# First attention of a four-part network: the four value passes of a head group stand in pairs, in two slots instead of four

## Chip, cores and metric

One NeuronCore of a Trainium2 chip runs the whole kernel in one launch. The metric is device time in microseconds (us); the median of the runs shown counts. Engines are called PE (TensorE, matrix products and transposes), DVE (VectorE), ACT (ScalarE), POOL (GpSimd) and SP (SyncE, which here issues DMAs). They run side by side, each through its own list of instructions in order, and wait for each other by semaphores.

## What is computed

The network has two blocks, each an attention and a feed-forward part, with a residual sum and a normalisation after each part. The change lies in the first attention alone: causal softmax attention over 4 batch entries, 512 positions, width 256, 16 heads of width 16, with rotary angles on the first four columns of each head.

```python
# x: (4, 512, 256)
qkv = x @ w_qkv + b_qkv                       # 16 heads of q, k, v, 16 wide each
q, k = rotate(q), rotate(k)                   # first 4 columns of each head
scores = where(causal, q @ k.T, -inf)
probs = softmax(scores)
attn = probs @ v                              # the value passes of this case
x = layernorm(x + attn @ w_out + b_out)
# then: the wave feed-forward part, a linear attention, six feed-forward blocks
```

## The kernel before

**Tiling.** A batch entry's 512 positions are four tiles of 128 (`RT` = 4). The heads are taken two at a time, in 8 pairs (`PAIRS`), and two pairs make a group of four heads (`GROUPS` = 4 of them). For each of the four entries, `entry(i, when)` of each engine walks through 8 pairs `p` with 4 slots `r` each, 32 slots in all; below (p,r) is a slot. `when` is "first" for entry 0, "loop" for entries 1 and 2, "last" for entry 3.

**One slot on PE.** `entry` (L954 on) issues, in this order: `score_pass(i, p, r)` (L835), two products, one for each head of the pair, over keys of tile `J_ORDER[r]`, so 512, 128, 384 and 256 columns in slots 0 to 3; `max_pass` (L824), the same two heads of the pair two further on, 128, 256, 384 and 512 columns, of which DVE takes row maxima; at most one `value_pass` (L848); in slot 1 `max_rows` (L858), a transpose of the negated maxima; then `use_work`, whatever the table `WORK_AT` has for the slot: transposes of q and k stacks (`stack`, L878), of the input (`x_T`), of the attention's output (`att_T`) or the normalised rows (`next_T`, all L943), a projection to q, k, v (`project`, L871) or the output projection (`out`, L887); and in slot 3 of even pairs `transpose_outputs` (L864). In some slots `keep_busy` (L952) adds products whose result nobody reads. In the last entry products that prepare the next part (L923, L929) take the place of some of the work.

**Value passes.** `value_pass(i, q, r)` multiplies the probabilities of key tile `J_ORDER[r]` by the values, for the four heads of group q, each head in its own 32 columns of the array: pass 0 has 512 columns, pass 1 128, pass 2 384, pass 3 256. They are called v0, v1, v2, v3 here. A pass is 8 matmuls in the trace (two rounds of four heads). All four add into one bank, `outputs`. v0 waits until ACT has copied the group before; each pass waits for `g_sel`, POOL's causal mask (`select`, L579) of slot r of the odd pair of its group. Group q is pairs 2q and 2q+1; its v0 and v1 stand in slots 2 and 3 of the odd pair, v2 and v3 in slots 0 and 1 of the even pair behind it (for the last group of an entry that is pair 0 of the next entry, and for the last group of all the end of the loop, where v2 and v3 stand together already).

**What orders the work around it.**
- Scores: ACT takes exponentials (L695) of each slot's two score products into `probs`; POOL masks them. A score pass waits until all but the last exponential of the slot before are done (in slot 0: all of them), since three banks are shared.
- Maxima: each head of the pair has one bank. The max pass of a slot waits, head by head, until DVE has taken the maximum (L1104) of the slot before. The maximum pass of slot (p,1) is followed on DVE by `take_rows` (L1118), whose rows SP sends by DMA to `heads_T`; `score_pass` of the next pair's slot 0 waits for that.
- `use_work` has one bank, `work`, and `max_rows`, `stack` and `transpose_outputs` share another, `exchange`. A use waits until its reader is done with the use before. The readers: ACT copies the stacks out (`copy_k` L682, `copy_q` L688) and takes the high part of transposes (`high`, L663 to L667); DVE takes the low part (`low`, L1141) and adds biases of projections (L1153). ACT also builds the next stack's high part (`stack_high`, L674 and L676), POOL its low part (`stack_low`, L585 and L587), and POOL rotates (L564 to L568).
- In slot 0 of even pairs the work is: pair 0 `stack`, pair 2 `att_T`, pair 4 `stack`, pair 6 `project`; in slot 3 of odd pairs: pair 1 `stack`, pair 3 `out`, pair 5 `stack`, pair 7 `project` (entry 0 has no `att_T` and no `out`).

Of the kernel before, what the change touches and what calls it, by code (L numbers as in the profile page):

```python
# [304 lines left out]
def work_table(when):  # L305

    table = {}
    for p, r, kind, arg in WORK_AT:
        if kind in PREVIOUS:
            used = when != "first"  # L310
        else:
            used = when != "last" if kind == "x_T" else of_entry(when, arg[0])
        if used:
            table[p, r] = (kind, arg)
    for p, r, kind, arg in {"first": FIRST_AT, "loop": (), "last": LAST_AT}[when]:
        table[p, r] = (kind, arg)
    return dict(sorted(table.items()))


def group_at(p, r, when):  # L320
    return r == RT - 1 and p % 2 == 0 and (p > 0 or when != "first")
# [39 lines left out]
def attention0(nc, A, g, top):  # L361
# [15 lines left out]
    GROUPS = H // 4  # L377
# [83 lines left out]
    def wait(eng, sem, count):  # L461

        if not isinstance(count, int) or count > 0:
            eng.wait_ge(sem, count)
# [341 lines left out]
    def _(pe):  # L806
        pe.wait_ge(s["ident_in"], 16)

        def max_pass(i, p, t, unit_at):

            if p % UP == 0:

                if unit_at[1] == "before":
                    pe.wait_ge(s["first_copied"], 2 * (t + 1))
                else:
                    key = ("stack", (1 if p else 2, t))
                    pe.wait_ge(s["work_read"], WORK.number(*unit_at, key) + 1)
                    pe.wait_ge(s["ex_read"], EXCHANGE.number(*unit_at, key) + 1)
            for o in range(2):
                n = (i * PAIRS + p) * 2 * RT + 2 * t + o  # L820
                rows = slice(o * SLOT, (o + 1) * SLOT)

                pe.wait_ge(s["v_max"], n + 1)
                pe.matmul(ps[:, o, 0:(t + 1) * P], heads_T[rows, p // UP, 0, p % UP, t * P:(t + 1) * P],  # L824
                          heads_T[rows, p // UP, 1, p % UP, 0:(t + 1) * P], start=True, stop=True).then_inc(s["p_max"], 1)

        def score_pass(i, p, r):
            j = J_ORDER[r]
            if r == 0:
                pe.wait_ge(s[f"m_row{p % 2}"], 32 * (i * (PAIRS // 2) + p // 2 + 1))  # L830

            wait(pe, s["a_exp"], ((i * PAIRS + p) * RT + r) * 2 - (0 if r == 0 else 1))
            for o in range(2):
                rows = slice(o * SLOT, (o + 1) * SLOT)
                pe.matmul(ps[:, score_bank(r, o), 0:COLS[j]], heads_T[rows, p // UP, 1, p % UP, j * P:(j + 1) * P],  # L835
                          heads_T[rows, p // UP, 0, p % UP, j * P:S], start=True, stop=True).then_inc(s["p_score"], 1)

        def value_pass(i, q, r):

            j = J_ORDER[r]  # L840
            if r == 0:
                pe.wait_ge(s["a_out"], i * GROUPS + q + 1)
                if q % 2 == 0:
                    pe.wait_ge(s["g_val"], 2 * RT * i + (q // 2 + 1) * RT)
            pe.wait_ge(s["g_sel"], (i * PAIRS + 2 * q + 1) * RT + r + 1)
            for h in range(4):
                rows = 2 * DH * h
                mm = pe.matmul(outputs[rows:rows + 2 * DH, j * P:S], val[:, j, 4 * q + h, :],  # L848
                               probs[:, h // 2, h % 2, OFF[j]:OFF[j] + COLS[j]],
                               start=(r == 0), stop=(r == RT - 1))  # L850
            if r == RT - 1:
                mm.then_inc(s["p_out"], 1)

        def max_rows(i, when, p, pair):

            pe.wait_ge(s["v_neg"], pair + 3)
            pe.wait_ge(s["ex_read"], EXCHANGE.number(i, when, ("neg", p)))
            pe.transpose(exchange[:, 0:P].bitcast(F32R), neg_max[:, :], ident_r[:, :]).then_inc(s["p_ex"], 1)  # L858

        def transpose_outputs(i, when, q):  # L860
            pe.wait_ge(s["a_out"], i * GROUPS + q + 2)
            pe.wait_ge(s["ex_read"], EXCHANGE.number(i, when, ("group", q if when != "after" else -1)))
            for t in range(RT):
                mm = pe.transpose(exchange[:, t * P:(t + 1) * P], out_T[:, t * P:(t + 1) * P], ident[:, :])  # L864
            mm.then_inc(s["p_ex"], 1)
# [84 lines left out]
        def keep_busy(bank, count):  # L950
            for _ in range(count):
                pe.matmul(bank, wout_h[:, 0, 0:P], wout_h[:, :, :].rearrange("p c d -> p (c d)"), start=True, stop=True)  # L952

        def entry(i, when):  # L954
            table = work_table(when)
            for p in range(PAIRS):
                for r in range(RT):
                    if (i, p, r) != (0, 0, 0):
                        score_pass(i, p, r)
                    if p + 2 < PAIRS:  # L960
                        max_pass(i, p + 2, r, (i, when))
                    elif when != "last":
                        max_pass(i + 1, p + 2 - PAIRS, r, (i, when))

                    if p % 2 and r >= 2:
                        value_pass(i, p // 2, r - 2)
                    elif p % 2 == 0 and r < 2 and p:
                        value_pass(i, p // 2 - 1, r + 2)
                    elif p == 0 and r < 2 and when != "first":
                        value_pass(i - 1, GROUPS - 1, r + 2)  # L970
                    row_next = r == 1 and (p < PAIRS - 1 or when != "last")

                    if row_next and p != 1:
                        max_rows(i, when, p + 1, i * PAIRS + p + 1)
                    if (p, r) in table:
                        use_work(i, when, *table[p, r])
                    if row_next and p == 1:
                        max_rows(i, when, p + 1, i * PAIRS + p + 1)
                    if group_at(p, r, when):
                        transpose_outputs(i, when, p // 2 - 1)  # L980
                    if (p, r) in KEEP_AT[when]:
                        count, use = KEEP_AT[when][p, r]
                        wait(pe, s["work_read"], WORK.number(i, when, use))
                        keep_busy(work, count)
# [47 lines left out]
        pe.wait_ge(s["g_ones"], 1)  # L1032
        pe.wait_ge(s["g_wout"], 1)
        entries(pe, entry)
        for r in range(2, RT):
            value_pass(B - 1, GROUPS - 1, r)
# [1616 lines left out]
```

## Time and profile before

| | us |
|---|---|
| median of 3 runs | 1064.11 (1063.26 to 1064.51) |
| the profiled execution's own time | 1064.57 |
| its span in the trace | 1062.8 |
| first attention's loops, from pair 0 of entry 0 to the last value pass | about 32 to 303 |
| PE busy over the span | 1001.7 (94%) |
| DVE, ACT, POOL busy | 748.1 (70%), 611.1 (57%), 373.8 (35%) |

Between span and time lie 1.8 us that the trace does not cover. PE's busy time counts a matmul from its dispatch to its modelled end, so that matmuls overlap in it and short waits hide in it; the distance from the start of one pass to the start of the next is the better measure of what a pass takes, and it is used below. A bracket at a row's end names the idle time of the engine ahead of it and what ended it.

### The profile page before, as it was taken

To read this page: it belongs to the slowest core of one execution; us is meant where nothing else is said; L and a number is where in the kernel's file an instruction comes from. 1 tells how busy PE (TensorE), PEld (TensorE's weight loads), DVE (VectorE), ACT (ScalarE), POOL (GpSimd) and SP (SyncE) were. 2 spreads that over 40 slices of the span, in tenths; PEclk is the share of its full clock that TensorE was granted. 3 is DMA by queue.
4 is the path that set the end of the run, shared out by engine and by line. 5 is a ranking of instruction groups with operands and counts; after the bars stand their busy time and mean duration, and the time that the engine had idled before them with its cause. 6 is when DMAs were issued, how large, how long until landed. Compare 5 with 4: busy or idle time off the path is not lost.

```text
span 1062.8 us, 18308 instructions
## 1 busy us (share of the span) xinstructions
PE 1001.7 (94%) x6627; PEld 836.2 (79%) x6627; DVE 748.1 (70%) x2042; ACT 611.1 (57%) x1177; POOL 373.8 (35%) x725
## 2 busy tenths in 40 slices
PE   6999999999998898889999999999999999999995
PEld 5555655556667897778989999998999999899995
DVE  5666787777639678967567767667776766677646
ACT  5566667564368576555556665456666545666640
POOL 4454474551221573553622233222223322222600
PEclk9899999999999999999999999999999999999998
DMA  7000010022110010022101011010101101010101
GB/s 247 22 2 21 4 41 1 22 67 74 60 45 4 1 34 9 1 100 80 60 1 41 3 38 41 1 41 1 40 2 40 40 2 40 1 41 1 52 29 40
DMA packets 29234, 36.91 MB, mean 35 GB/s; under 512 B 1780, under 2 KB 26584, under 8 KB 29144
## 3 DMA queue, kind: packets, MB, share of 16 engines
q1 hardware_dynamic: 24872, 31.28, 9.1%
q10 hardware_dynamic: 4272, 4.46, 1.4%
q8 instruction: 53, 0.87, 0.3%
q14 instruction: 37, 0.30, 0.1%
HBM read 31.40 MB, written 4.20 MB: 33 GB/s over the span
## 4 chain that ended last, share of the span: by engine, by line
PE 54%; DVE 5%; ACT 1%; POOL 1%; issue 1%; DMA 1%; SPq 0%; DVEq 0%; POOLq 0%; ACTq 0%
PE ps L1894 25%; PE ps L1877 24%; PE ps L1849 2%; PE ps L1767 1%; PE ps L1818 1%; DVE ln_stats L86 1%; DMA mlp_b<-L_ffn_LN_B 1%; DVE ln_stats L2256 0%; ACT xn L2016 0%; ACT x_b L2037 0%; DVE att L2339 0%; PE ps L1809 0%; DVE xT_l L2298 0%; PE ps L1720 0%; DVE ln_mv L91 0%
## 5 line engine op out<-in xcount | busy, mean ns | idle before, releaser
L2115 ACT ACTIVATE G<-ps,bias_col 128x512 f32<-128x512 f32 x192 | 135.5, 706 | 186.3 <-PE ps L1877 176.8
L1894 PE MATMUL ps<-w_h,G_h 128*128 128x256 f32 x736 | 208.2, 283 | 0.0
L1894 PE MATMUL ps<-w_h,G_l 128*128 128x256 f32 x736 | 207.9, 282 | 0.0
L1894 PE MATMUL ps<-w_l,G_h 128*128 128x256 f32 x736 | 207.8, 282 | 0.0
L2387 DVE TENSOR_TENSOR G_l<-G,G_h 128x512 fp32r<-128x512 f32 x192 | 155.2, 815 | 59.9 <-ACT G_h L2116 59.9
L1696 POOL TENSOR_TENSOR x_a<-xn,mlp_g 128x1024 f32<-128x1024 f32 x20 | 67.6, 3379 | 344.8 <-DVE xn L2417 344.8
L695 ACT ACTIVATE probs<-ps 128x512 f32<-128x512 f32 (+3 forms) x256 | 98.3, 441 | 98.2 <-PE ps L835 97.4
L1877 PE MATMUL ps<-xT_h,w_h 128*128 128x512 f32 x384 | 152.0, 396 | 1.1 <-issue 1.1
L1877 PE MATMUL ps<-xT_h,w_l 128*128 128x512 f32 x384 | 150.6, 392 | 0.0
L1877 PE MATMUL ps<-xT_l,w_h 128*128 128x512 f32 x384 | 150.4, 392 | 0.0
L1104 DVE CUSTOM_DVE_ANT_0 ps<-ps,q_mask 128x128 f32<-128x128 f32 (+3 forms) x256 | 120.7, 512 | 30.6 <-PE ps L824 30.1
L1894 PEld LDWEIGHTS ps<-w_h,G_h 128*128 128x128 f32 x736 | 139.9, 190 | 0.7
L1894 PEld LDWEIGHTS ps<-w_h,G_l 128*128 128x128 f32 x736 | 140.3, 191 | 0.0
L1894 PEld LDWEIGHTS ps<-w_l,G_h 128*128 128x128 f32 x736 | 139.5, 190 | 0.8
L2116 ACT ACTIVATE G_h<-ps,bias_col 128x512 fp32r<-128x512 f32 x192 | 135.0, 703 | 0.0
L2401 DVE TENSOR_TENSOR rsum<-ps,x_a 128x1024 f32<-128x1024 f32 x23 | 28.2, 1225 | 105.4 <-PE ps L1894 105.4
L579 POOL TENSOR_SCALAR_AFFINE_SELECT probs<-probs 128x256 f32<-128x256 f32 x128 | 53.1, 416 | 99.1 <-ACT probs L695 98.4
L1877 PEld LDWEIGHTS ps<-xT_h,w_h 128*128 128x128 f32 x384 | 72.1, 188 | 16.2 <-issue 1.5
L1877 PEld LDWEIGHTS ps<-xT_h,w_l 128*128 128x128 f32 x384 | 72.1, 188 | 15.7
L1877 PEld LDWEIGHTS ps<-xT_l,w_h 128*128 128x128 f32 x384 | 72.2, 188 | 14.9
L2381 DVE TENSOR_TENSOR xT_l<-hs,xT_h 128x512 fp32r<-128x512 f32 x40 | 77.1, 1954 | 2.3 <-ACT xT_h L2101 1.1
L824 PE MATMUL ps<-heads_T 64*128 64x128 f32 (+3 forms) x256 | 56.6, 353 | 5.9 <-DVE top_score L1104 5.7
(303 smaller groups left out, 2120.7 us busy)
## 6 DMA issues: line engine op xcount, KB each, us to landing
w_raw<-L_ffn_W_T SPq DMA_DIRECT2D x12, 1024.0 KB, 5.5
hs<-L_attn_hidden_states SPq DMA_DIRECT2D x8, 512.0 KB, 4.0
x_kept<-hs SPq DMA_DIRECT2D x4, 512.0 KB, 3.9
w_raw<-x_kept SPq DMA_DIRECT2D x2, 1024.0 KB, 5.4
out<-xn SPq DMA_DIRECT2D x3, 512.0 KB, 2.9
w_raw<-L_ffn_ent_w_T SPq DMA_DIRECT2D x1, 1024.0 KB, 9.9
w_raw<-L_ffn_ent_pw SPq DMA_DIRECT2D x1, 1024.0 KB, 12.3
heads_T<-neg_rows SPq DMA_DIRECT2D x64, 2.0 KB
```

The source lines that it names most:

```text
L579: pool.affine_select(diagonal, diagonal, [[0, 2], [1, P]], ALU.is_ge, 0.0, base=0, channel_multiplier=-1).then_inc(s["g_sel"], 1)
L695: act.activation(probs[:, p % 2, o, OFF[j]:OFF[j] + COLS[j]], ps[:, score_bank(r, o), 0:COLS[j]], ACT.Exp).then_inc(s["a_exp"], 1)
L824: pe.matmul(ps[:, o, 0:(t + 1) * P], heads_T[rows, p // UP, 0, p % UP, t * P:(t + 1) * P], heads_T[rows, p // UP, 1, p % UP, 0:(t + 1) * P ...
L1104: v.tensor_tensor_reduce(ps[:, o, 0:(t + 1) * P], ps[:, o, 0:(t + 1) * P], q_mask[:, S - (t + 1) * P:S], 1.0, MASKED, ALU.add, ALU.max, to ...
L1696: pool.tensor_tensor(g.x_a[:, rows, :], xn[:, b % 2, :, :], bcast(g.mlp_g[:, i, :], 1, [P, RT, D]), ALU.mult).then_inc(feed["g_mul"], 1)
L1877: mm = pe.matmul(ps[:, hidden_bank(i, n), :], w[:, c, f * P:(f + 1) * P], x[:, b, c, :], start=(k == 0), stop=(k == 5))
L1894: mm = pe.matmul(ps[:, 4 + t // 2, (t % 2) * D:(t % 2 + 1) * D], x[b % 2][f][:, t * P:(t + 1) * P], w2_chunk(w, f), start=(k == 0), stop=( ...
L2115: act.activation(G32[n % 4], bank, ACT.Gelu, bias=bias)
L2116: act.activation(G_h[b % 2][f], bank, ACT.Gelu, bias=bias).then_inc(feed["a_g"], 1)
L2381: v.tensor_tensor(g.xT_l[:, b, c, :], src, g.xT_h[:, b, c, :].bitcast(F32), ALU.subtract).then_inc(feed["v_T"], 1)
L2387: v.tensor_tensor(G_l[b % 2][f], G32[n % 4], G_h[b % 2][f].bitcast(F32), ALU.subtract).then_inc(feed["v_gl"], 1)
L2401: v.tensor_tensor(g.rsum[:, :, :], ps[:, 4:6, :].rearrange("p a (b c) -> p (a b) c", c=D), g.x_a[:, b * RT:(b + 1) * RT, :], ALU.add).then ...
```

## The change

The call sites of `value_pass` in PE's `entry` move. v1 goes from slot 3 of the odd pair to slot 2, right behind v0; v3 goes from slot 1 of the even pair to slot 0, right behind v2. The passes themselves, their waits, all other engines' programs and the passes at the end of the loop stay as they are.

```diff
-                    if p % 2 and r >= 2:
-                        value_pass(i, p // 2, r - 2)
-                    elif p % 2 == 0 and r < 2 and p:
-                        value_pass(i, p // 2 - 1, r + 2)
-                    elif p == 0 and r < 2 and when != "first":
-                        value_pass(i - 1, GROUPS - 1, r + 2)
+                    if p % 2 and r == 2:
+                        value_pass(i, p // 2, 0)
+                        value_pass(i, p // 2, 1)
+                    elif p % 2 == 0 and r == 0 and p:
+                        value_pass(i, p // 2 - 1, 2)
+                        value_pass(i, p // 2 - 1, 3)
+                    elif p == 0 and r == 0 and when != "first":
+                        value_pass(i - 1, GROUPS - 1, 2)
+                        value_pass(i - 1, GROUPS - 1, 3)
```

## Rows read from the trace of the kernel before

**Rows 1.** Busy time by stretch, entry 1: us; busy by engine; granted clock; DMA, GB/s.

```profile
95.50:158.30 62.80, 59.00 (x443) 36.84 (x441) 49.81 (x189) 41.56 (x106) 34.91 (x96) 1.00 0.06 18
```

**Rows 2.** Waits of PE, 46 to 303.4 us: total us, times, longest.

```profile
PE ps L824 <- DVE top_score L1104: 4.5, 9, 0.9
PE ps L835 <- ACT probs L695: 2.8, 6, 0.7
```

**Rows 3.** Timeline, entry 1, (1,2) to (2,1): start, us, engine, line, operation, tiles, [idle].

```profile
106.91 1.07 PE L848 MATMUL ps<-probs,val 128*32 128x512 f32 x8
...
107.93 0.38 PE L835 MATMUL ps<-heads_T 64*128 64x256 f32 x2
...
108.16 0.54 PE L824 MATMUL ps<-heads_T 64*128 64x512 f32 x2
...
108.63 0.43 PE L848 MATMUL ps<-probs,val 128*32 128x128 f32 x8
108.98 0.54 PE L878 MATMUL ps<-ident_r,k_stack 128*128 128x128 f32 x4
...
109.87 0.14 DVE L1104 DVE_READ_ACCUMULATOR2_ANT top_score<- 128x1 f32 x1
109.87 0.49 PE L835 MATMUL ps<-heads_T 64*128 64x512 f32 x2
...
110.21 0.22 PE L824 MATMUL ps<-heads_T 64*128 64x128 f32 x2
110.35 0.85 PE L848 MATMUL ps<-probs,val 128*32 128x384 f32 x8
...
111.14 0.66 PE L943 MATMUL ps<-ident,att 128*128 128x128 f32 x4
...
112.15 0.64 PE L848 MATMUL ps<-probs,val 128*32 128x256 f32 x8
...
112.46 0.69 DVE L1141 TENSOR_TENSOR att_l<-ps,att_h 128x512 fp32r<-128x512 f32 x1 [1.27 <-ACT att_h L665]
112.72 0.28 PE L858 MATMUL ps<-ident_r,neg_max 128*128 128x128 f32 x1
...
113.20 0.44 PE L871 MATMUL ps<-wqkv_h,x_h 128*128 128x384 f32 x1 [0.21 <-DVE att_l L1141]
```

**Rows 4.** Timeline of PE, the end of entry 3: v1 and v2 without work between.

```profile
301.49 1.07 PE L848 MATMUL ps<-probs,val 128*32 128x128 f32 x16
...
301.73 0.51 PE L848 MATMUL ps<-probs,val 128*32 128x384 f32 x4
```

**Rows 5.** Timeline, entry 1, (4,0) and (4,1): ACT's copy and the next row transpose.

```profile
128.70 0.59 ACT L688 ACTIVATE heads_T<-ps 128x512 fp32r<-128x512 f32 x1
...
129.44 0.28 PE L858 MATMUL ps<-ident_r,neg_max 128*128 128x128 f32 x1
```

**Rows 6.** Timeline of PE, entry 0, score pass of (4,0).

```profile
64.24 0.49 PE L835 MATMUL ps<-heads_T 64*128 64x512 f32 x2 [0.24 <-ACT probs L695]
```

**Rows 7.** Timeline of PE, entry 3, work of (4,0).

```profile
261.07 3.72 PE L923 MATMUL ps<-w_raw 128*128 128x256 f32 x16 [0.38 <-DVE rsum L1182]
```

**Rows 8.** Timeline of PE, entry 1: max pass of (5,3), project of (6,1).

```profile
141.00 1.01 PE L824 MATMUL ps<-heads_T 64*128 64x512 f32 x2 [0.94 <-DVE top_score L1104]
...
146.72 0.41 PE L871 MATMUL ps<-wqkv_h,x_h 128*128 128x384 f32 x1
```

**Rows 9.** Timeline, v0 and select of (7,1) in entry 1, score of (0,2) in entry 2.

```profile
155.01 1.06 PE L848 MATMUL ps<-probs,val 128*32 128x512 f32 x8
...
155.64 0.40 POOL L579 TENSOR_SCALAR_AFFINE_SELECT probs<-probs 128x256 f32<-128x256 f32 x1
...
162.08 0.19 PEld L835 LDWEIGHTS ps<-heads_T 64*128 64x128 f32 x2 [0.17 <-ACT probs L695]
```

**Rows 10.** Busy time by stretch, (6,0) and (6,1) of entries 1 and 2.

```profile
143.09:147.94 4.85, 4.85 (x38) 3.00 (x37) 2.15 (x11) 2.29 (x6) 1.91 (x6) 1.00 0.01 2
206.22:212.45 6.23, 6.23 (x40) 3.61 (x39) 2.09 (x10) 2.30 (x6) 1.93 (x6) 0.75 0.01 3
```

## The prediction

> **What bounds the kernel now.** I read first the busy times of one loop entry [rows 1]: PE is busy for 59.00 of 62.80 us, DVE for 49.81, ACT for 41.56. So PE's list sets the pace, but with little to spare on the others. Then the waits of PE [rows 2]: they are few, and the largest are its max passes on DVE (4.5 us in 9) and its score passes on ACT (2.8 us in 6). Last the timeline of PE beside the engines that read its banks [rows 3]: there it shows that much of PE's order is timed to the readers. The reader should look there not at busy time but at which pass stands between a product and the next product that needs the same bank.
>
> The change takes no instruction away and adds none. It can bring or cost time in three ways: two passes next to each other may be cheaper than two apart; a pass that moves may fill a wait; or it may have been filling one, which is then bare.
>
> **What a joined pass costs.** From start to the next start v0 takes 1.02 us (106.91 to 107.93), v1 0.35 (108.63 to 108.98), v2 0.79 (110.35 to 111.14) and v3 0.57 (112.15 to 112.72) [rows 3]. At the end of the loop v1 and v2 already stand together, and there v1 takes 0.24 (301.49 to 301.73) [rows 4]. So the first of two joined passes is some 0.12 shorter. It is the one place of its kind; v0 before v1 and v2 before v3 are not seen, and I take 0.12 for them, bounds 0 and 0.15. The Trainium skill speaks against it: "TensorE: Matmul & The Clock Gate", section "Measured speedup vs the span model", says that a weight load overlaps running matmuls only where its rows of the array differ, and all value passes use all rows. By that rule the join would save nothing; the 0.24 disagrees, and the rule's time is a rival below.
>
> **Odd pair.** Behind v0 now follows v1, then the score and max pass of slot 3. Both start 0.35 - 0.12 = 0.23 us later, the work of slot 3 at least 0.12 earlier. The exponentials, the mask and the maximum of slot 3 come 0.23 later with them. **Even pair.** v3 now stands ahead of the work of slot 0, which comes 0.57 - 0.12 = 0.45 later than v2's shift alone; in slot 1 it is gone, so that everything from the row transpose on could come as early as before or earlier, if its bank is free. No DMA is moved; the row DMA behind the maximum of the even pair's slot 1 comes up to 0.45 later and has some microseconds until its score pass. What counts is who reads the delayed work, so I go by group (1 to 4), each in entries 0 to 3.
>
> **Group 1, pairs 1 and 2.** v1 can start at 106.91 + 1.02 - 0.12 = 107.81, the score pass of (1,3) at 108.16, its max pass at 108.39. That pass took 0.47 to v1 (108.16 to 108.63), as its second half waited for DVE. A pair of 512 columns whose halves go together takes 0.34 (the score pass, 109.87 to 110.21). So the stack work of (1,3) starts at 108.73, not 108.98, and the score pass of (2,0) at 108.73 + 0.89 = 109.62, its max pass could at 109.96. But DVE ended the last maximum of (1,3) at 109.87 + 0.14 = 110.01 and now ends it 0.23 later, at 110.24. So the second half of that max pass waits, and v2 starts at about 110.50 (110.35 before), some 0.25 behind the release. v3 follows at 111.17, and the `att_T` work starts at 111.74, not 111.14: +0.60. From that work to the projection of (2,1) runs a chain without slack: transposes, ACT's `high`, DVE's `low`, then the projection, which waits for the low part now already (0.21 idle), 2.06 us in all [rows 3]. v3 filled that time. The projection thus starts at 113.80, +0.60, three times (entries 1 to 3; in the last the `low` delays the maximum and with it the row DMA instead): +1.80. Entry 0 has a short transpose there, whose reader is done in time: +0.05. Without the new wait on DVE it would be +0.45 each: bounds 0.45 to 0.65.
>
> **Group 2, pairs 3 and 4.** In the loop entries `out` in (3,3) is long enough to cover DVE; v2 comes 0.12 + 0.17 (a max half that no longer waits) = 0.29 earlier, the stack work of (4,0) 0.45 - 0.29 = 0.16 later. ACT's second copy of that stack ends at 128.70 + 0.59 = 129.29, and the row transpose of (4,1), which writes the same bank, stands at 129.44 [rows 5], just behind v3. Now v3 is not there and the copy is the wait: +0.16, twice, +0.32. In entry 0 there is no work in (3,3): the score pass of (4,0) already waits for the exponentials of (3,3) [rows 6], which come 0.23 to 0.30 later; so v2 +0.30, the work +0.75, the row transpose about +0.70. In entry 3 the work of (4,0) waits for DVE in any case (0.38 idle [rows 7]); v3 moves into that wait and leaves the slot behind it: -0.49. Sum +0.53, bounds 0 and 1.0.
>
> **Group 3, pairs 5 and 6.** DVE is in a normalisation, and the max pass of (5,3) waits 0.94 for it [rows 8]. v1 behind the pass moves ahead of it, into the wait: -0.35. The project work of (6,0) comes 0.45 - 0.35 = 0.10 later; the project of (6,1) shows no wait [rows 8] and keeps most of the gain, as the DVE addition that it waits for then ends only just ahead of it: -0.27 in entries 1, 2 and 3. In entry 0 the stack of (5,3) waits for POOL, and little is gained: -0.05. Sum -0.86, bounds -1.5 and 0.
>
> **Group 4, pair 7 and pair 0 of the next entry.** Joined, v1 could start at 155.01 + 1.02 - 0.12 = 155.91, but its mask ends at 155.64 + 0.40 = 156.04 [rows 9]: it waits 0.15 to 0.20, and v2 comes 0.09 earlier, not 0.29. So the stack work of (0,0) comes 0.45 - 0.09 = 0.36 later. ACT copies that stack, builds the next one and only then takes the exponentials of (0,1), for which the score pass of (0,2) waits now already (0.17) [rows 9]: +0.36, twice, and +0.34 behind entry 0. After the last entry v3 has to follow the mask of (7,3), whose score pass now comes behind v1: +0.23, and double that if PE is at half clock as in this profile; I take +0.45. Sum +1.51, bounds 0.9 and 1.8.
>
> **Sum.** 1.85 + 0.53 - 0.86 + 1.51 = 3.03 us. The bounds of the groups add up to 0.8 and 3.9; joins that save nothing come on top. The rest of the kernel starts behind the last value pass and moves with it. The profiled execution, 1064.57 us, would come to 1067.6; it lies 0.46 over the median, and from the median 1064.11 it is **1067.2 us**, 0.28% more.
>
> **Rivals.** (a) The covers hold: the readers of the work in even slot 0 have 0.45 us or more to spare, ACT and DVE being idle for a third and a fifth of an entry [rows 1]. Then 31 joins bring 31 x 0.12 = 3.7 and the maxima waits of slot 3 that v1 now fills some 2.0 more: 1058.4 us, faster. It speaks for it that in group 3 such slack exists; against it the idle times in groups 1 and 4, with the reader's name beside them [rows 3, 9]. It decides at 0.45 us of slack in groups 1, 2 and 4.
> (b) The clock. The same work, (6,0) and (6,1), took 4.85 us at full clock in entry 1 and 6.23 in entry 2, where the granted clock was 0.75 on average (a part of it at 1.2 GHz instead of 2.4), right behind the 0.94-like wait of (5,3): 1.38 us for one such drop [rows 10]. v1 inside that wait and the shift of everything may take a drop away: 1065.8, no difference; the new bare waits of groups 1 and 4 may add one or two: 1068.6 to 1070.0. I see no reason to prefer either.
> (c) Joined passes are no cheaper, as if a pass's weights could not be loaded beside the matmuls of the pass before. Then the work of even slot 0 comes up to 0.24 later in each group, on the path in groups 1, 2 and 4 (10 places, about 0.2 each) and partly in group 3: +2.3, 1069.5. This is what the rule of the Trainium skill named above would give; the one joined pair [rows 4] is against it.
> (d) That the change does not do what it says, v0 and v1 standing apart because v1's mask is late, can be only in pair 7, and is in the sum.
>
> **How the numbers follow.** A run's spread and other effects of some 0.2% (2.1 us) can't be told from no change. My forecast, 1064.9 to 1068.5 by itself, has 0.50, of which 0.12 lie within 0.2% (up to 1066.2). (a) has 0.11, faster. (b) has 0.17 with fewer drops, same, and 0.13 with more, slower. (c) has 0.09, slower. That makes faster 0.11, same 0.12 + 0.17 = 0.29, slower 0.38 + 0.13 + 0.09 = 0.60. The range leaves out (a) and the far end of (b): 1062.5 to 1070.6.
>
> **What would show it.** In the profile after: the joined v0 should take 0.90 to v1, v2 0.67 to v3. In (2,1) of entries 1 and 2 the projection should show near 0.9 us of idle time behind DVE's low part, the score pass of (0,2) a wait of 0.6 or more on ACT, the row transpose of (4,1) one of about 0.3 on ACT, and the max pass of (5,3) should keep a wait on DVE of some 0.7. The wait of the max passes of (1,3) and (3,3) should be gone, and that of (2,0) be new. I am wrong if the projection of (2,1) starts no later than 2.85 us behind v2, as before (3.30 forecast), if PE's waits on ACT and DVE in the loops do not grow by some 4 us together, or if the number of stretches at half clock differs from that of before.

## The result: 0.25% slower, and where it went

| | kernel before | changed kernel |
|---|---|---|
| median, us | 1064.54 (1061.17 to 1066.06, 11 runs) | 1067.37 (1065.47 to 1068.71, 11 runs) |
| ratio | | 1.0025, 95% interval 1.0015 to 1.0034 |
| profiled execution: time and span, us | 1064.57 and 1062.8 | 1066.52 and 1064.8 |

The change costs 2.8 us; 3.1 were forecast, with 1062.5 to 1070.6 as the range.

The page of the changed kernel has the same number of instructions and, but for PE's overlap, the same busy times:

```profile
span 1064.8 us, 18308 instructions
## 1 busy us (share of the span) xinstructions
PE 998.8 (94%) x6627; PEld 839.0 (79%) x6627; DVE 747.9 (70%) x2042; ACT 611.8 (57%) x1177; POOL 374.5 (35%) x725
```

PE is busy for 2.9 us less and the span is 2.0 us longer: in these two executions the time went into waits. PE's waits in the loops, 46 to 306 us (total us, times, longest), of which [rows 2] show the first and the third before, with 4.5 and 2.8:

```profile
PE ps L824 <- DVE top_score L1107: 4.3, 10, 0.7
PE ps L858 <- ACT heads_T L688: 4.0, 7, 1.0
PE ps L835 <- ACT probs L695: 3.5, 7, 0.7
PE ps L864 <- ACT heads_T L688: 2.4, 6, 0.6
PE ps L871 <- DVE att_l L1144: 1.6, 2, 0.8
```

What has grown most is the second: the row transpose (L858) waits for ACT's copy of the stack from the same bank, 4.0 us in 7 places; without the one long wait in the last entry, which the kernel before had too (0.8), that is 3.0 in 6: (4,1) of entries 0 to 2 and (0,1) of entries 1 to 3, 0.50 or 0.51 us each. The kernel before has none of these six. The projection that waits for DVE's low part of `att_T` went to 1.6 us in 2 places; it had 0.21 before in each [rows 3].

The timeline of PE from (1,2) to (2,1) in entry 1 of the changed kernel, to be laid beside [rows 3]:

```profile
108.09 1.28 PE L848 MATMUL ps<-probs,val 128*32 128x512 f32 x16
109.30 0.39 PE L835 MATMUL ps<-heads_T 64*128 64x256 f32 x2
109.53 0.40 PE L824 MATMUL ps<-heads_T 64*128 64x512 f32 x2
109.94 0.53 PE L878 MATMUL ps<-ident_r,k_stack 128*128 128x128 f32 x4
...
111.22 0.50 PE L835 MATMUL ps<-heads_T 64*128 64x512 f32 x2 [0.41 <-DMA heads_T<-neg_rows]
111.56 0.22 PE L824 MATMUL ps<-heads_T 64*128 64x128 f32 x2
111.71 1.28 PE L848 MATMUL ps<-probs,val 128*32 128x384 f32 x16
112.92 0.66 PE L943 MATMUL ps<-ident,att 128*128 128x128 f32 x4
...
113.94 0.28 PE L858 MATMUL ps<-ident_r,neg_max 128*128 128x128 f32 x1
114.99 0.44 PE L871 MATMUL ps<-wqkv_h,x_h 128*128 128x384 f32 x1 [0.78 <-DVE att_l L1144]
```

A row with x16 is two passes back to back. From v0 to the projection it is 114.99 - 108.09 = 6.90 us, where it was 113.20 - 106.91 = 6.29 [rows 3]: +0.61. The reader should see both halves of the change in it: the stack work comes sooner after v0 (1.85 us, was 2.07), and the `att_T` work later after v2 (1.21, was 0.79). From that work to the projection it is 2.07 us in this kernel and 2.06 in the one before. Nothing in that chain got slower; it starts later, and v3, which used to fill it, is already done.

In (4,1) of entry 1 the row transpose now waits for ACT (timeline, all engines), and in (0,1) of the next entry too, where the score pass behind it keeps its old wait of 0.17:

```profile
130.60 0.59 ACT L688 ACTIVATE heads_T<-ps 128x512 fp32r<-128x512 f32 x1
...
131.34 0.25 PE L858 MATMUL ps<-ident_r,neg_max 128*128 128x128 f32 x1 [0.51 <-ACT heads_T L688]
...
163.48 0.25 PE L858 MATMUL ps<-ident_r,neg_max 128*128 128x128 f32 x1 [0.51 <-ACT heads_T L688]
...
164.16 0.19 PEld L835 LDWEIGHTS ps<-heads_T 64*128 64x128 f32 x2 [0.17 <-ACT probs L695]
```

And the max pass of (5,3) waits less, since v1 went into that wait (0.94 before [rows 8]):

```profile
142.88 1.01 PE L824 MATMUL ps<-heads_T 64*128 64x512 f32 x2 [0.72 <-DVE top_score L1107]
```

### The profile page after: what moved, and what is told of

Its sections match the earlier page's. It is cut to its first block, busy times and chain, and to the rows that moved or that the text cites. A ratio compares the mean times of both kernels' runs of the same rounds, so it can differ in the third digit from the quotient of the medians.

```text
span 1064.8 us, 18308 instructions
## 1 busy us (share of the span) xinstructions
PE 998.8 (94%) x6627; PEld 839.0 (79%) x6627; DVE 747.9 (70%) x2042; ACT 611.8 (57%) x1177; POOL 374.5 (35%) x725
## 4 chain that ended last, share of the span: by engine, by line
PE 54%; DVE 5%; ACT 1%; issue 1%; POOL 1%; DMA 1%; SPq 0%; DVEq 0%; POOLq 0%; ACTq 0%
PE ps L1897 25%; PE ps L1880 24%; PE ps L1852 2%; PE ps L1770 1%; PE ps L1821 1%; DVE ln_stats L86 1%; DMA mlp_b<-L_ffn_LN_B 1%; DVE ln_stats L2259 0%; ACT xn L2019 0%; ACT x_b L2040 0%; DVE att L2342 0%; PE ps L1812 0%; PE ps L1723 0%; DVE xT_l L2301 0%; DVE ln_mv L91 0%
```

## The experiments

**Theory:** each piece of work in even slot 0 is read back by ACT or DVE through a bank that PE needs again in slot 1; v3 used to fill that time, and now delays its start. **Rivals:** the odd pair is to blame, whose exponentials and maxima come later; two passes in one slot are too much; it is the clock.

The table gives, in us, by how much each kernel is later than the one before at each group: the time from the start of the score pass of slot 2 of the odd pair to that of slot 2 of the even pair, less the same in the first trace of the kernel before. A star is a stretch with half clock on one side; values with + behind them are taken against a second trace of the kernel before, whose clock was full there. Group 2 of entry 0 is left out: every trace but that of v2+v3 alone has half clock in it; what can be read there at full clock is told below.

| group, entry | forecast | changed | changed, again | v0+v1 alone | v2+v3 alone | v3 behind the work | by group |
|---|---|---|---|---|---|---|---|
| 1, 0 | 0.05 | 0.06 | 0.04 | 0.21 | -0.14 | 0.18 | 0.02 |
| 1, 1 | 0.60 | 0.60 | 0.56 | 0.22 | 0.45 | 0.16 | -0.01 |
| 1, 2 | 0.60 | 0.59 | 0.59 | 0.16 | 0.43 | 0.17 | -0.01 |
| 1, 3 | 0.60 | 0.28 | 0.29 | 0.13 | 0.15 | 0.18 | 0.00 |
| 2, 1 | 0.16 | 0.11 | 0.11 | -0.31 | 0.41 | -0.32 | -0.30 |
| 2, 2 | 0.16 | 0.05 | 0.10 | -0.37 | 0.41 | -0.37 | -0.34 |
| 2, 3 | -0.49 | -0.49 | -0.50 | -0.01 | -0.50 | -0.01 | -0.50 |
| 3, 0 | -0.05 | 0.06 | 0.07 | -0.02 | 0.07 | -0.01 | -0.02 |
| 3, 1 | -0.27 | -0.26 | * | -0.32 | 0.05 | -0.35 | -0.36 |
| 3, 2 | -0.27 | * | -0.29+ | * | 0.05+ | * | -0.37+ |
| 3, 3 | -0.27 | -0.25 | -0.25 | -0.36 | 0.11 | -0.35 | -0.34 |
| 4, 0 | 0.34 | 0.43 | 0.38 | -0.04 | 0.44 | -0.04 | 0.01 |
| 4, 1 | 0.36 | 0.44 | 0.47 | 0.00 | 0.52 | 0.00 | 0.01 |
| 4, 2 | 0.36 | 0.42 | 0.41 | -0.02 | 0.42 | -0.01 | -0.02 |

### The odd pair alone

The diff is against the changed kernel: v2 and v3 stand apart again.

```diff
 if p % 2 and r == 2:
     value_pass(i, p // 2, 0)
     value_pass(i, p // 2, 1)
-elif p % 2 == 0 and r == 0 and p:
-    value_pass(i, p // 2 - 1, 2)
-    value_pass(i, p // 2 - 1, 3)
-elif p == 0 and r == 0 and when != "first":
-    value_pass(i - 1, GROUPS - 1, 2)
-    value_pass(i - 1, GROUPS - 1, 3)
+elif p % 2 == 0 and r < 2 and p:
+    value_pass(i, p // 2 - 1, r + 2)
+elif p == 0 and r < 2 and when != "first":
+    value_pass(i - 1, GROUPS - 1, r + 2)
```

> Only v0 and v1 are joined, in slot 2 of the odd pair; v2 and v3 stay apart as in the kernel before. My theory: the loss comes from v3 ahead of the work of even slot 0, so without that it is gone. By group, as shift of the score pass of slot 2 of the even pair: group 1 +0.15 in entries 1 to 3 (the new wait of the max pass of (2,0) on DVE), about 0 in entry 0; group 2 +0.30 in entry 0, -0.29 in entries 1 and 2, 0 in entry 3; group 3 -0.35 in entries 1 to 3; group 4 -0.1 each, and +0.3 at the end. Sum about -0.9 us. Rival 1: the loss comes from the odd pair, whose exponentials, masks and maxima of slot 3 come later: then this kernel loses the 2 to 3 us by itself. Rival 2: joined passes are no cheaper: -0.9 would be about +0.3.

Measured: median 1062.18 us, ratio to the kernel before 0.9979 (0.9969 to 0.9989), so 2.2 us faster (1.2 to 3.3). The odd pair does not carry the loss. The projection of (2,1) starts 114.72 - 111.87 = 2.85 us behind v2, as before, with its old wait:

```profile
111.87 0.85 PE L848 MATMUL ps<-probs,val 128*32 128x384 f32 x8
112.66 0.66 PE L943 MATMUL ps<-ident,att 128*128 128x128 f32 x4
113.67 0.64 PE L848 MATMUL ps<-probs,val 128*32 128x256 f32 x8
...
114.72 0.44 PE L871 MATMUL ps<-wqkv_h,x_h 128*128 128x384 f32 x1 [0.21 <-DVE att_l L1142]
```

The groups follow the expectation (0.13 to 0.22, -0.31 and -0.37, -0.32 and -0.36, 0). With the end of the loop (+0.2) they add up to a gain of less than 1 us, though, and the median moved by 2.2, at least 1.2. The granted clock of whole runs, on record for each, accounts for much of the rest. Over the 21 runs of the kernel before that stand beside this kernel's ten, a higher mean clock goes with a shorter time: at 0.981 seven runs took 1065.0 us on average, at 0.984 two took 1060.6 and 1062.3. Eight of the ten runs of this kernel have 0.984, and they took 1062.1 on average, no less than those two. So at equal clock no gain over the kernel before is shown in the times. Why this kernel's runs have the higher clock more often is open; it may be its own doing.

### The even pair alone

Again against the changed kernel: v0 and v1 stand apart.

```diff
-if p % 2 and r == 2:
-    value_pass(i, p // 2, 0)
-    value_pass(i, p // 2, 1)
+if p % 2 and r >= 2:
+    value_pass(i, p // 2, r - 2)
 elif p % 2 == 0 and r == 0 and p:
     value_pass(i, p // 2 - 1, 2)
     value_pass(i, p // 2 - 1, 3)
```

> Only v2 and v3 are joined, in slot 0 of the even pair; v0 and v1 stay apart. My theory: each even slot 0's work comes 0.45 us later. Group 1 +0.45 in entries 1 to 3, -0.1 in entry 0; group 2 +0.40 in entries 0 to 2, -0.5 in entry 3; group 3 -0.12; group 4 +0.45 three times. Sum about +3.0 us, as much as or more than the whole change, since the odd half of the change no longer gives anything back. Rival 1 (the odd pair is to blame): about 0 or, by the cheaper joins, -1.9. The projection of (2,1) in entry 1 should wait longer for DVE's low part: 0.6 to 0.7 us idle instead of 0.21.

Measured: median 1067.72 us, ratio 1.0033 (1.0017 to 1.0049), 3.5 us slower (1.8 to 5.2); the groups of the table add up to +2.9. This half carries the whole loss and more. The six waits of the row transpose on ACT's copy are all here (0.50 or 0.51 each), and in the kernel with the odd pair alone none is. From v2 to the projection it is 114.34 - 111.06 = 3.28 us:

```profile
111.06 1.28 PE L848 MATMUL ps<-probs,val 128*32 128x384 f32 x16
112.27 0.65 PE L943 MATMUL ps<-ident,att 128*128 128x128 f32 x4
...
114.34 0.44 PE L871 MATMUL ps<-wqkv_h,x_h 128*128 128x384 f32 x1 [0.78 <-DVE att_l L1143]
```

Group 3, where the project has slack, loses 0.05 to 0.11, not -0.12 as expected: the slack there is a little less than the 0.45 of the delay.

### v3 in the same slot, behind the work

Against the changed kernel:

```diff
 elif p % 2 == 0 and r == 0 and p:
     value_pass(i, p // 2 - 1, 2)
-    value_pass(i, p // 2 - 1, 3)
 elif p == 0 and r == 0 and when != "first":
     value_pass(i - 1, GROUPS - 1, 2)
-    value_pass(i - 1, GROUPS - 1, 3)
...
 if (p, r) in table:
     use_work(i, when, *table[p, r])
+if p % 2 == 0 and r == 0 and p:
+    value_pass(i, p // 2 - 1, 3)
+elif p == 0 and r == 0 and when != "first":
+    value_pass(i - 1, GROUPS - 1, 3)
```

> As the changed kernel (v0 and v1 joined, v3 in even slot 0), but v3 stands behind the work of that slot, not ahead of it. Only the order of v3 and one piece of work differs from the changed kernel. My theory: the readers of the work start before v3 and v3 covers them again, so the loss of the even pair is gone: about -0.9 us against before, like the kernel with only the odd pair joined, and some 3 to 4 us less in the loops than the changed kernel. Rival: what costs is that slot 1 no longer holds v3, or that slot 0 holds two passes: then it loses 2 to 3 us like the changed kernel.

Measured: median 1062.03 us, ratio 0.9987 (0.9975 to 0.9999), so 1.4 us faster than the kernel before (0.1 to 2.7; the medians, 1062.03 and 1064.49, lie 2.5 apart), where the changed kernel has 1.0025. This is the sharpest test: slot 0 still holds two value passes and slot 1 none, and only the order of v3 and one use of the bank differs. The loss is gone, and so are the six waits of the row transpose; the groups are those of the odd pair alone, to 0.03 in most. In (2,0) the work now stands right behind v2, v3 behind it, and the projection again 113.94 - 111.08 = 2.86 us behind v2:

```profile
111.08 0.85 PE L848 MATMUL ps<-probs,val 128*32 128x384 f32 x8
111.87 0.66 PE L943 MATMUL ps<-ident,att 128*128 128x128 f32 x4
112.45 0.64 PE L848 MATMUL ps<-probs,val 128*32 128x256 f32 x8
...
113.94 0.45 PE L871 MATMUL ps<-wqkv_h,x_h 128*128 128x384 f32 x1 [0.21 <-DVE att_l L1146]
```

### The changed kernel and the kernel before once more

Both unaltered, for one more trace each.

> The changed kernel once more, unaltered, for one look. My theory: the shifts of the passes against the kernel before, slot by slot, come out the same to a few hundredths of a us wherever the clock is full; only the stretches at half clock fall elsewhere, by one or two, so that the time may differ by 1 to 2 us from the look before. Rival: the stretches at half clock come from the change's new waits and fall on the same slots again.

Measured: 1067.50 us. The groups repeat to 0.05 at full clock. The stretches at half clock do not: the same work, (6,0) and (6,1), ran at half clock for a while in entry 2 of the first trace and in entry 1 of the second. Busy time by stretch, first trace, then second (the last three columns are granted clock, DMA share, GB/s):

```profile
144.70:149.60 4.90, 4.88 (x40) 3.23 (x39) 2.37 (x13) 2.22 (x6) 1.65 (x7) 1.00 0.00 2
208.50:215.10 6.60, 6.59 (x40) 4.29 (x39) 2.46 (x13) 2.29 (x6) 1.77 (x7) 0.74 0.01 2
```

```profile
145.30:151.80 6.50, 6.49 (x40) 3.90 (x39) 2.44 (x13) 2.27 (x6) 1.73 (x7) 0.74 0.01 1
209.40:214.30 4.90, 4.88 (x41) 3.19 (x40) 2.72 (x12) 2.31 (x6) 1.88 (x4) 1.00 0.01 3
```

> The kernel before once more, unaltered, for one look. My theory: slot for slot the same as in its first look to a few hundredths of a us at full clock, except in entry 0's start, behind DMAs; the stretches at half clock may fall elsewhere and move the time by 1 to 2 us. Rival: they fall on the same slots.

Measured: 1060.39 us, 4.2 less than the profiled execution of the same kernel. Between the two traces the groups differ by 0.01 at full clock, except 0.14 in group 1 of entry 1; nearly the whole difference lies in the clock: (6,0) and (6,1) of entry 2 ran at full clock and took 1.45 us less, the beginning of entry 3 1.3 less, its middle 0.8 more, the loop's end 1.3 less; 0.7 us of the rest came behind the first attention. So stretches at half clock move without any change of the program, and one time against one time says little about 2 us.

### A version by group

v1 joins v0 only in pair 3 of the loop entries and in pair 5; v2 and v3 stand together only in pair 4 of the last entry; all else as before.

```diff
-if p % 2 and r >= 2:
-    value_pass(i, p // 2, r - 2)
+joined = p == 5 or (p == 3 and when == "loop")
+if p % 2 and r == 2:
+    value_pass(i, p // 2, 0)
+    if joined:
+        value_pass(i, p // 2, 1)
+elif p % 2 and r == 3 and not joined:
+    value_pass(i, p // 2, 1)
+elif (p, when) == (4, "last"):
+    if r == 0:
+        value_pass(i, 1, 2)
+        value_pass(i, 1, 3)
```

> A version put together group by group: v1 is joined to v0 only where DVE holds the max pass of slot 3 and no reader loses by it (pair 3 of entries 1 and 2, pair 5 of all entries); v2 and v3 are joined only in pair 4 of the last entry, where the work behind them waits for DVE anyway; all else as in the kernel before. My theory, at full clock: -0.3 twice (pair 3), -0.35 three times (pair 5), -0.5 once (pair 4 of the last entry), no group slower: -2.2 us, 1062.3. Rival: what the kernels with v0 and v1 joined gained came from fewer stretches at half clock, not from these groups: then no difference to before, 1064.5.

Measured: median 1060.94 us, ratio 0.9964 (0.9951 to 0.9978), the lowest median of all. The table's column adds up to -2.2, as expected from the groups; the median moved by 3.8 (2.3 to 5.2). The rival, that the gain is the clock's alone, does not hold: at the same mean granted clock, 0.981, three runs of this kernel took 1061.1 us on average and four of the nine runs of the kernel before beside it 1064.5. The 1.2 us of that difference that the groups do not show stay open. In the profiled executions of the two kernels, 1060.84 and 1064.57 us, more than that lies outside the first attention: from the last value pass to the end of the span the same program took 757.5 us here and 759.4 in the first trace of the kernel before. Here is the gain of pair 5, v1 behind v0 and the shorter wait:

```profile
138.02 1.28 PE L848 MATMUL ps<-probs,val 128*32 128x512 f32 x16
140.34 1.01 PE L824 MATMUL ps<-heads_T 64*128 64x512 f32 x2 [0.72 <-DVE top_score L1113]
```

## Why the prediction was right

**The join.** Forecast 0.12 shorter. A pair of v0 and v1 takes 109.30 - 108.09 = 1.21 us, apart 1.02 + 0.35 = 1.37; v2 and v3 take 112.92 - 111.71 = 1.21, apart 0.79 + 0.57 = 1.36: 0.15 to 0.16. It was sized a little too small; 0.15 was the upper of its bounds. To v3 the joined v2 takes 0.67, as forecast, and v0 to v1 0.88 (0.90 forecast). Rival (c), that joined passes are no cheaper, is refuted by every joined pair that ran at full clock without a wait: all of them took 1.21 or 1.22 us. The rule of the Trainium skill that the prediction names stands on the page "TensorE: Matmul & The Clock Gate" in the section "The mechanism", not in the one named there; by it the join would save nothing, and the trace disagrees. In the pair of (2,0), v3's first weight load starts at 112.38 us, beside v2's last matmuls, whose modelled ends lie at 112.54 to 112.56.

**Group 1.** Forecast 0.60 in entries 1 to 3; 0.60, 0.59 and, by the table, 0.28. The chain `att_T`, ACT, DVE, projection is as told: v2 to projection 3.28 us, 3.30 forecast. The odd part is right in size (0.13 to 0.22 with v0 and v1 alone, 0.15 in the sum) but in entry 1 its cause is another: the score pass of (2,0) came early enough to meet the row DMA (0.41), ahead of the wait on DVE that was forecast. The row DMA was looked at only where the change moves it, not where PE comes to it sooner. It already held that pass a little in the kernel before, by 0.14 more in the second trace, against which entry 1 is 0.46 later. In entry 3 there is no projection in (2,1), and the table's end point lies ahead of the other half of the delay: the max pass of (2,2), just behind it, waits 0.60 for DVE's maximum and 0.32 before. From the score pass of (1,2) to that of (3,0) of this entry the second traces of the two kernels, both at full clock, take 10.99 (changed) and 10.42 us (before): 0.57 later, as forecast. The long wait for the row DMA there (1.46) stands in only one of the two traces of the kernel before.

**Group 2.** Forecast 0.16 twice and -0.49; 0.11, 0.05 to 0.10 and -0.49. In entry 0 0.70 was forecast. There the clock is full again behind v0: from the score pass of (3,3) to the projection of (4,1) it is 68.81 - 63.33 = 5.48 us, before 68.07 - 63.02 = 5.05, so 0.43 later; and v1 beside v0 puts that score pass back by 1.21 - 1.02 = 0.19. That makes some 0.62. The score pass of (4,0) waits for the exponentials as forecast (0.61, was 0.24), and the row transpose for the copy (0.51).

**Group 3.** Forecast -0.27 three times; -0.26, -0.29 and -0.25.

**Group 4.** Forecast 0.34 and twice 0.36; 0.43, 0.44 and 0.42. The place of the wait was named wrongly: not the score pass of (0,2) waits longer but the row transpose ahead of it, for an earlier copy of the same chain on ACT (0.51), and the score pass keeps its 0.17. The size holds, since both hang on the same work. The mis-sized term is the odd part, -0.09 forecast: v0 to v2 takes 3.79 us, 3.81 before, as the second half of the max pass of (0,0) now waits a little for DVE too.

**Sum.** The forecast terms come to 3.03 (over the median of 1064.11 that is 1067.1, not 1067.2), and the bounds of the groups add up to 0.8 and 4.8, not 3.9; both lie within the range given. Measured, the groups of the table (-0.29 in entry 2 of group 3) make 1.75; with 0.57 in place of 0.28 for group 1 of entry 3, some 0.62 for group 2 of entry 0, and 0.2 at the loop's end at full clock, as the kernel with v0 and v1 alone has it, it is 2.04 + 0.62 + 0.2 = 2.86. The medians differ by 2.83.

**The signs.** PE's waits on ACT and DVE in the loops grew from 13.1 to 17.6 us, by 4.5 (some 4 forecast). The projection of (2,1) waits 0.78 (0.9 forecast), the row transpose of (4,1) 0.51 (0.3 forecast). Stretches at half clock in the loops are five in the first trace of either kernel, but three in the second of the kernel before and five in the second of the changed one: their number differs between executions of one kernel, so this sign could not decide.

**Rivals.** (a), the covers hold, is refuted in groups 1, 2 and 4 and true for most of group 3 and for pair 4 of entry 3, where it had been said. (b), the clock, is real in single runs, up to 4 us, and it is not clear of the medians either. The eleven runs of the changed kernel have a mean clock of 0.978 to 0.981, while nine of the 21 later runs of the kernel before have 0.982 or more. At equal clock the two differ by less: 1067.2 against 1065.0 on average at 0.981 (4 and 7 runs), 1066.8 against 1065.4 at 0.980 (6 and 4). So a part of the 2.83 may be the clock's, and that it meets the sum of the passes' delays to 0.03 is luck. The mechanism rests on the waits and on the three kernels that take the change apart.

## What to carry to other kernels

In a list written out by hand, a short independent pass between two uses of one bank is cover, even where the busy times show PE as the bound: before it moves, find who reads the bank, and measure from the producer's start to the next user's start. A pass may move ahead of a wait that exists anyway, as v1 in pair 5 or v3 in the last entry's pair 4; put behind the product that others read, it cost nothing here even in the same slot. Joining passes of one tiling saved 0.15 us at full clock each time, less than the 0.45 that one piece of work lost by standing behind them.

## What the runs showed of the hardware

Two passes of 32-column tiles that follow each other take 0.15 us less (1.21 against 1.36 to 1.37) than with other matmuls between them, the same for 512 and 128 columns as for 384 and 256. And the stretches at half clock (1.2 instead of 2.4 GHz) of one unaltered kernel fell on other slots in another execution, those in (6,0) and (6,1) costing 1.4 to 1.7 us, while the groups at full clock came back to 0.05 us or better, but for 0.14 in one that meets a row DMA. A difference below 2 us in such a kernel is better read from the passes' starts than from a time; where times are compared, the mean granted clock of each run belongs beside them, since 0.981 and 0.984 lay 3 to 4 us apart in the runs of one kernel.
